# Group 0's first gates by TensorE, projection weights in three turns, and a new order of the first two groups

## The reference, cut to what matters

```python
x = x + tanh(g_xattn) * xattn(ctx, layernorm(x))        # 64 sequences of 128 tokens, 77 context tokens, width 128
h = layernorm(x)
logits = normalize(h) @ normalize(sim) - sigmoid(gates)  # 16 experts
w = softmax(where(mask > 0, relu(logits), -inf))         # mask: logits > 0, or the two largest
q, k, v = [sum_e w[:, e] * (h @ p[e]) for p in (q_proj, k_proj, v_proj)]
o = softmax(q @ k.T / sqrt(128)) @ v                     # within a sequence
x = x + tanh(g_ffn) * sum_e w[:, e] * (o @ o_proj[e])
```

## Time and profile before

| | us |
|---|---|
| median of 3 runs | 800.32 |
| lowest and highest | 799.54, 801.37 |
| the profiled execution | 799.99 |
| its span | 798.1 |
| TensorE busy | 776.1 (97%) |
| VectorE busy | 607.2 (76%) |
| GpSimd busy | 483.0 (61%) |
| ScalarE busy | 433.8 (54%) |
| mean granted clock of TensorE | 0.987 of 2.4 GHz |

### The profile page before, as it was taken

One profiled execution on the slowest core, in us unless ns is written; L12 is line 12 of the kernel. 1 busy time (PEld: TensorE's weight loads), 2 busy tenths in 40 slices (PEclk: granted clock), 3 DMA queues, 4 the chain that ended last, 5 costly groups with the idle time before them and its releaser, 6 DMA issues.

```text
span 798.1 us, 13995 instructions
## 1 busy us (share of the span) xinstructions
PE 776.1 (97%) x3999; PEld 418.1 (52%) x3999; DVE 607.2 (76%) x2037; ACT 433.8 (54%) x1129; POOL 483.0 (61%) x703
## 2 busy tenths in 40 slices
PE   7489999999999999999999999999999999999998
PEld 6445545555455555545555554555555455544444
DVE  2977787878787787778777787877878786775648
ACT  5554645556555655655565565456556555544445
POOL 3276657674746757474675747567574755765534
PEclk9789999999999999999999999999999999999999
DMA  6564476563655636365563636546364654543100
GB/s 192 136 216 159 162 219 174 169 209 94 209 161 164 189 106 204 97 210 167 151 191 106 202 109 209 166 150 186 101 207 116 208 160 139 163 135 116 53 14 28
DMA packets 97476, 122.57 MB, mean 154 GB/s; under 512 B 14611, under 2 KB 69111, under 8 KB 97399
## 3 DMA queue, kind: packets, MB, share of 16 engines
q1 hardware_dynamic: 96679, 121.59, 49.6%
q10 hardware_dynamic: 720, 0.08, 0.1%
HBM read 97.32 MB, written 24.31 MB: 152 GB/s over the span
## 4 chain that ended last, share of the span: by engine, by line
PE 88%; DVE 5%; DMA 2%; POOL 1%; ACT 1%; issue 1%; SPq 0%; DVEq 0%; ACTq 0%; POOLq 0%
PE acc_q L1380 20%; PE acc_k L1380 20%; PE acc_v L1380 20%; PE y L1409 9%; PE oT_p L1409 9%; PE m L1489 2%; PE m L1553 2%; DVE x_all L1175 1%; PE oT_p L1641 1%; PE m L1480 1%; PE m L1539 1%; DMA stage<-in_L_ffn_q_proj_dram 1%; PE m L1469 1%; POOL zq L658 1%; PE m L1529 1%
## 5 line engine op out<-in xcount | busy, mean ns | idle before, releaser
L658 POOL TENSOR_TENSOR zq<-zq_full,zq 128x512 f16<-128x512 f32 x256 | 297.8, 1170 | 222.4 <-ACT zq L743 222.2
L743 ACT ACTIVATE zq<-zq_full 128x512 f16<-128x512 f32 x256 | 160.1, 636 | 224.1 <-DVE zq_full L1145 224.0
L1175 DVE SCALAR_TENSOR_TENSOR x_all<-y,w_out,x_all 128x128 f32<-128x128 f32 x356 | 122.2, 343 | 96.1 <-issue 69.5
L1380 PE MATMUL acc_q<-zq,w_hi 128*128 128x512 f16 x510 | 193.3, 379 | 1.0 <-POOL zq L658 1.0
L1380 PE MATMUL acc_k<-zq,w_hi 128*128 128x512 f16 x510 | 193.2, 379 | 0.0
L1380 PE MATMUL acc_v<-zq,w_hi 128*128 128x512 f16 x510 | 193.2, 379 | 0.0
L1145 DVE TENSOR_TENSOR zq_full<-wq_bc,x2T_p 128x512 f32<-128x512 f32 x256 | 167.8, 668 | 2.5 <-DMA wq_bc<-w_rows 1.7
L1175 DVE SCALAR_TENSOR_TENSOR x_all<-oT_p,w_out,x_all 128x128 f32<-128x128 f32 x356 | 121.5, 341 | 0.0
L673 POOL TENSOR_TENSOR x_all<-stage,x_all 128x128 f32<-128x128 f32 x240 | 100.4, 456 | 19.8 <-DVE x_all L1175 13.3
L1380 PE MATMUL acc_q<-zq,w_lo 128*128 128x512 f16 x255 | 96.6, 379 | 0.0
L1380 PE MATMUL acc_v<-zq,w_lo 128*128 128x512 f16 x255 | 96.6, 379 | 0.0
(11 more groups left out here) (253 smaller groups left out, 1091.4 us busy)
## 6 DMA issues: line engine op xcount, KB each, us to landing
wq_bc<-w_rows SPq DMA_DIRECT2D x128, 512.0 KB, 4.5
blk_rows<-stage SPq DMA_DIRECT2D x26, 256.0 KB, 2.7
stage<-blk_rows SPq DMA_DIRECT2D x104, 64.0 KB, 2.0
blk_rows<-v_blk SPq DMA_DIRECT2D x15, 256.0 KB, 2.0
v_mix<-blk_rows SPq DMA_DIRECT2D x60, 64.0 KB, 2.9
blk_rows<-pc_blk SPq DMA_DIRECT2D x15, 256.0 KB, 4.1
pcT<-blk_rows SPq DMA_DIRECT2D x60, 64.0 KB, 2.0
out_dram<-x_all SPq DMA_DIRECT2D x15, 256.0 KB, 6.7
```

The source lines that it names most:

```text
L658: nc.gpsimd.tensor_tensor(zq[:, 1, e % Z_SLOTS, :], zq_full[:, e % F_SLOTS, :], zq[:, 0, e % Z_SLOTS, :], ALU.subtract).then_inc(zq_lo_poo ...
L743: nc.scalar.activation(zq[:, 0, e % Z_SLOTS, :], zq_full[:, e % F_SLOTS, :], ACT.Copy).then_inc(zq_hi_done, 1)
L1175: nc.vector.scalar_tensor_tensor(out=rows(x_all, g, b0 + b), in0=bank[:, tok(j)], scalar=w_out[:, g % 2, e, b0 + b:b0 + b + 1], in1=rows(x ...
L1380: last = nc.tensor.matmul(acc[m][:], w[:, m, s, :], zq[:, half, s % Z_SLOTS, :], start=(s == 0 and n == 0), stop=(s == E - 1 and n == 2))
```

## The change

1. *Gates by TensorE.* For the experts 0 and 1 of group 0 (BY_PE = 2) `gate_diagonal` on VectorE builds a 128x512 tile with the gates on the diagonal of each 128x128 block, in wq_bc's slot 0, and `gate_spread` multiplies it by a matrix of ones: the gates then stand in every partition, in the banks m0 and oT_p. `zq_scale` reads them there, with x2T from SBUF. SyncE's spread of pair 0 is left out.
2. *Weights in three turns.* Q, K, V are split for experts 0 to 3, 4 to 9 and 10 to 15 (PARTS) in instructions of their own; the last turn is in pass 0. TensorE waits for each turn where its first expert comes, and `first_expert` does its three w_hi products ahead of the w_lo ones.
3. *The head's order.* The cross-attention of group 0 goes ahead of the transposes of contexts 1 to 3; Q's weights are loaded ahead of those contexts, x of group 1 ahead of V's weights. The statistics of group 1's first norm come sooner, and the gates of group 0 are ahead of the weights' scales. More, shorter runs of `keep_busy` stand between the head's products. `att_product(1)` and `x1_add(1)` go into pass 0.
4. *Pass 0.* The second norm of group 1 moves (x2_norm at step 3, its transpose and gates two steps later than before: GATES_LATE = 3); `second_rstd(1)`, `second_norm(1)` and `first_rstd(2)` on POOL move behind more of group 0's zq_low; x_norm(2) goes to step 4 and its transpose to bank m1.
5. *O's weights* are looked through and split later: maximum at step 10 instead of 2, shared at 11 and 12 instead of 4 and 7, w_hi at step 14 instead of 9, w_lo at step 3 of pass 1 instead of step 11 of pass 0. In pass 1 the copy of oT goes ahead of that step's zq_high.

The diff, cut:

```diff
+BY_PE = 2
+PARTS = ((0, 4), (4, 10), (10, 16))
+GATES_LATE = 3
...
         def late(i):
-            return 1 if i == 0 else 0
+            return GATES_LATE if i == 0 else 0
...
-        MAX_AT, SHARE_AT = (0, 2), ((0, 4), (0, 7))
-        HIGH_AT = (0, 9)
-        LOW_AT = (0, 11)
+        MAX_AT, SHARE_AT = (0, 10), ((0, 11), (0, 12))
+        HIGH_AT = (0, 14)
+        LOW_AT = (1, 3)
...
                 sp.wait_ge(kq_in, 16 * 2)
+                load_weights(Q, q_proj)
...
-                load_weights(Q, q_proj)
                 load_weights(K, k_proj)
+                load_x(1)
                 load_weights(V, v_proj)
-                load_x(1)
...
-                for j in range(W_SLOTS):
+                for j in range(BY_PE // 2, W_SLOTS):
                     spread_q(0, j)
...
                 first_rstd(1)
-                for e in range(LEAD - 1):
+                for e in range(LEAD):
                     zq_low(0, e)
-                second_rstd(1)
-                zq_low(0, LEAD - 1)
-                first_rstd(2)
...
+                    if i == 0 and s == 2:
+                        second_rstd(1)
                     for g, e in zq_at(i, s):
                         zq_low(g, e)
-                    if s == 1 and i < 2:
+                    if s == (3 if i == 0 else 1) and i < 2:
                         second_norm(g2)
+                    if i == 0 and s == 3:
+                        first_rstd(2)
...
+                    if i == 1 and s == Y_FIRST:
+                        oT_high(0)
+                    if i == 0 and s == 3:
+                        x2_norm(1)
                     for g, e in zq_at(i, s):
                         zq_high(g, e)
...
-                    if s == (3 if i == 0 else 0) and has(g1):
+                    if s == (4 if i == 0 else 0) and has(g1):
                         x_norm(g1)
...
+                    if i == 0 and s in (1, 2, 3):
+                        weight_high((Q, K, V)[s - 1], 2)
-                    if s == 1 and i < 2:
+                    if s == 1 and i == 1:
                         x2_norm(g2)
...
+            def gate_diagonal(e):
+
+                wait(dve, w_ready, 1)
+                nc.vector.tensor_tensor(wq_bc[:, 0, e].rearrange("p (b t) -> p b t", b=G),
+                                        ident[:].unsqueeze(1).broadcast_to([P, G, P]),
+                                        w_new[:, 0, e].unsqueeze(2).broadcast_to([P, G, P]),
+                                        ALU.mult).then_inc(w_diag_done, 1)
...
+                if g == 0 and e < BY_PE:
+                    wait(dve, x2T_sb, 1)
+                    wait(dve, w_spread_ps, e + 1)
+                    nc.vector.tensor_tensor(zq_full[:, e, :], SPREAD_BANKS[e][:], x2T[:],
+                                            ALU.mult).then_inc(zq_full_done, 1)
+                    return
...
+                    if i == 0 and s == 0:
+                        x1_add(1)
+                        second_stats(1)
+                        weight_low(V, 1)
+                    if i == 0 and s == 2:
+                        first_stats(2)
+                    if i == 0 and s in (3, 4, 5):
+                        weight_low((Q, K, V)[s - 3], 2)
...
-                wait(pe, logit_read, cap(g))
+                if g == 2:
+                    wait(pe, x1_done, 2)
...
+            def gate_spread(e):
+
+                pe.wait_ge(w_diag_done, e + 1)
+                pe.wait_ge(logit_read, 1)
+                nc.tensor.matmul(SPREAD_BANKS[e][:], ones[:], wq_bc[:, 0, e], start=True,
+                                 stop=True).then_inc(w_spread_ps, 1)
...
+                px_transpose(0)
+                att_product(0)
                 for g in range(1, PRE + 1):
                     ctx_transpose(g)
...
+                keep_busy(6)
+                gate_spread(0)
+                gate_spread(1)
                 px_transpose(1)
-                att_product(1)
+                keep_busy(2)
...
+                    if i == 0 and s == 0:
+                        att_product(1)
```

More of the change, by code:

```diff
@@ L971, in body @@
                         kxT_out(g1)
[L972 to L975 removed]
+                    if s == Y_FIRST and i > 1 and has(gc):
+                        oT_high(gc)
                     if s == 10 - sooner(i) and has(g1):
@@ L1376, in experts @@
                 for m in (Q, K, V):
+                    for part, (first, _) in enumerate(PARTS):
+                        if (i, s) == (0, first):
+                            pe.wait_ge(hi_done[m], part + 1)
+                            pe.wait_ge(lo_done[m], part + 1)
                     if s == 0:
```

109 lines of the change are left out of this document (62 added, 47 removed).

## The result

The changed kernel takes **810.23 us** (median of 4 executions, 808.72 to 811.24) against 800.83 (4 executions, 799.54 to 801.37) on the same chip: ratio 1.0118, 95% interval 1.0094 to 1.0142. Slower, as forecast, but by 9.4 us and not 5, and outside the range. The profiled execution took 809.29 us, 9.30 more than the profiled one of before.

The account below looks back on a forecast made before the run. TensorE bounds the kernel, busy 776.1 of 798.1 us, with time to win only in the first 43 us. Terms -7.1, +1.0, +5.4, +3.2, +1.4, +0.5, +0.7 sum to +5.1: 805.0 us, chance 0.50, range 799.8 to 807.5.

Parts of the forecast that it names:

- to expert 0: Head and gates by TensorE: gates ready at 32.3, spread 0.9 and diagonal 0.6 each; expert 0 at 36.1, 7.1 us earlier.
- 5 to 6: Norm of group 1: second_rstd(1) behind zq_low 5, TensorE idle 1.6 us for x2_norm(1); expert 6 at 53.9, 5.2 earlier.
- 6 to 7: Norm of group 2: first_rstd(2) late on POOL, TensorE waits 4.5 us in xn_transpose(2); expert 7 only 0.7 earlier.
- 7 to 12: Out's weights: maximum behind group 1's gate chain, waits of 2.7 and 1.2 us; expert 12 at 74.8, 2.5 later.
- I take 0.7, since VectorE's chain, not TensorE, sets expert 12: Clock behind the 4.5 us wait of TensorE: a fall to half clock, costed at 0.7 us.
- The upper bound of 1.7: Highest cost of the clock's fall, for a stretch with 3.4 us of matmuls; the other upper bound was 1.2.
- The sentence on the Trainium skill's rule: Throttled state is the default and activity releases it; by that the wait costs its full 1.7, the sum 1.0 higher.
- An operation of VectorE with both inputs in SBUF and a zq_low don't run together: VectorE and POOL among group 0's zq_low: the later one waits; expert 0 waits 0.5 and 1.5 for first w_lo pieces.
- rival (a): VectorE and POOL overlap freely, the exclusion doesn't bite: 800.5 us, up to 801.7 with the clock; chance 0.20.
- rival (b): Lead survives xn_transpose(2) if first_rstd(2) is done by 54.2, before second_norm(1): -1.5 to -3.5, 797.5 us; chance 0.13.
- Rival (c): Clock falls in the head too, or the pair by DMA lands late: +6.5 to +8, 807 us; chance 0.17.
- Rival (d): Diagonal brings nothing, as V's first w_lo piece and the pair by DMA set the pace; changes no time, no chance given.

Follow-up runs that it names:

- e6: Changed kernel with the w_lo pieces for Q, K and V reading x2T_p in PSUM instead of w_hi in SBUF; 807.92 us, ratio to before 1.0092.
- e1: Changed kernel with 10 short float32 products ahead of TensorE's wait for x2 of group 1 and 20 ahead of that for xn of group 2; 807.61 us.
- e2: Changed kernel with second_rstd(1) and first_rstd(2) earlier on POOL, x2_norm(1) and x_norm(2) one step earlier on ScalarE; 802.70 us, ratio to before 1.0030.
- e3: Changed kernel with the four places of out's weights (maximum, share, high half, low half) as before; 804.14 us, ratio to before 1.0044.
- e5: Changed kernel with the edits of e2 and e3 together; 802.08 us, ratio to before 1.0020.
- e10: e5 without the diagonals and float32 spreads, all of group 0's gates by DMA as before; 803.38 us, ratio to before 1.0043.
- e9: e5 with the transpose of wmax, and out's share, high and low half, two steps later; 801.30 us, ratio to before 1.0008.
- e13: e9 with the six later w_lo pieces computing 128 of 768 columns, the other low halves zero; 797.79 us, ratio to before 0.9973.
- e14: e9 with GATES_LATE = 2, second_norm(1) one step sooner and the last w_lo pieces one later; 800.27 us, ratio to before 0.9997.
- e12: e9 with 27 more short float32 products filling TensorE's waits in the head, among the experts and in group 2; 800.84 us, ratio to before 1.0013.
- e11: Kernel before with the early activation of oT for group 0 and 46 more short float32 products in the head; 801.81 us, ratio to before 1.0019.
- e4: Changed kernel with 12 more short float32 products in the head, ahead of px's transpose, the attention product and the contexts' transposes; 809.82 us, ratio to before 1.0115.
- e8: e5 with each weight's halves split whole, in one turn of 16 experts instead of three; 804.34 us, ratio to before 1.0056.

## Why the prediction was right in sign and wrong in size

By its own steps, walk against the two profiles (us, minus is earlier than before):

| step | walk | measured | what failed |
|---|---|---|---|
| to expert 0 | -7.1 | -6.15 | gates 0.7 later than 32.3, a spread 1.12 for 0.9, a diagonal 0.65 |
| expert 0 to 1 | +1.0 | +0.77 | |
| 1 to 5 | -0.5 | -0.58 | |
| 5 to 6 | +1.4 | +2.98 | wait 2.5 for 1.6, second_rstd(1) held up by w_lo (e6: +1.59); clock 0.4 (e1: +2.57) |
| 6 to 7 | +4.5 | +5.24 | xn of group 2 comes later still, second_norm(1) 2.2 for 1.57; not the clock (e1: +5.23) |
| 7 to 12 | +3.2 | +4.64 | expert 7 at half clock, 4.79 (e1, at full clock: +2.99) |
| 12 to group 1 | +1.4 | +1.48 | |
| to group 2 | +0.5 | +0.99 | xnT late by 1.7 for 1.4; oT gave back 0.8 |
| clock | +0.7 | in the steps | fell three times, not once |
| sum | +5.1 | +9.37 | |

The miss of 4.3 us is thus 0.95 in the head, 1.6 and 0.7 at the two norms, 1.4 behind expert 7 and 0.3 in the other steps, less the 0.7 that the walk had set aside for the clock. e1 and e6 put their share of it between expert 0 and group 2 at 1.4 us for the clock and 1.7 for the exclusion, from one profile each.

*Right*, and shown by a run that undoes each: the lead dies in the norms (e2: 7.5 us of the median come off with the order of the norms), and at out's weights (e3: 6.1 us). The two overlap and don't add (8.2 together), so neither figure is a share of the loss. The exclusion of VectorE and POOL is real (e6), and group 2 carries the lag to the end. The places, and most durations, were those of the walk.

*Wrong: the clock.* The step "I take 0.7, since VectorE's chain, not TensorE, sets expert 12" failed. The runs show 1.4 to 2.6 us in its place (e1), for two falls among the experts. The upper bound of 1.7 took a stretch of 3.4 us of products at half clock, a length that no row shows; behind the second wait it was 5.7 (62.81 to 68.51). There TensorE was itself the chain: the logits of group 1 ride on expert 7, and VectorE stood idle for 8.2 us until they came. The reading behind the term was off as well: before's clock was not at 1.00 until 28.85, its trace has 0.50 from 12 to 15 us too. The sentence on the Trainium skill's rule ("TensorE: Matmul & The Clock Gate", section "What's actually happening") gave a sum 1.0 higher; the trace lies nearer to it than to mine, though not even it reaches the result.

*Wrong: what w_lo holds up.* "An operation of VectorE with both inputs in SBUF and a zq_low don't run together" was applied to zq_low alone. The power and the products of the norms on POOL, four elements wide, wait in the same way: 1.0 us on second_rstd(1), directly in the wait for x2(1), which became 2.5, and 0.6 on second_norm(1), in the chain to xn of group 2. With the exclusion off (e6) the step from expert 5 to 6 is +1.59, near the walk's +1.4.

*Wrong: the head*, by 0.95. The terms for the diagonal and the spread were near. In the profiles with this head expert 0 starts between 36.5 and 39.2, depending on where the half clock falls (last section), a fall that the walk did not have.

*Wrong: the price of rival (a)*, 800.5. With the exclusion switched off for Q, K and V (e6) the time is 807.9. The rival's walk let everything else fall into place; it did not.

*Right for a wrong reason: rival (b)* named the one place that decides, first_rstd(2) ahead of second_norm(1). e2 makes that true, the lead passes to expert 7 (20.68 us behind expert 0, 18.25 in before, so that 1.7 of the lead is left there), and the time is 802.7, not 797.5. What is left was not in the rival: e2 still has out's weights behind the gate chain (with them back, e5, 802.1) and VectorE's extra work.

*Rival (c)*, the clock falling in the head too, was the true case as far as it went (0.68 to 0.83 from 15 to 22 us), but its 807 was 3 short for the reasons above. *Rival (d)* falls: with the later steps mended, the kernel without the diagonals (e10) is 1.3 us slower than the one with them (e5).

Of what would show it right, the longest wait stood in the transpose of xn (3.5 instead of 4.5), 1.9 ahead of the transpose of wmax, none above 1 on oT, two zq_low took 3.63, and the clock stood at 0.50 around 63.

*What stays open*: of the 5.6 us that e9 takes longer than before from expert 0 to group 2, e13 removes 2.3, e14 0.3; the rest is not pinned to one cause. Nor is the scatter of the times of e5 and e12, though the start of expert 0 alone moves by 2.6 us between profiles (last section).

## What to carry to other kernels

A lead on the bounding engine is worth what the feeding engines can follow: compare each feeder's busy time from the new start to the next stage with what it was, before costing the lead. Where a change moves a small operation behind large ones on another queue, its whole chain counts, and a wait of 2 to 3 us on TensorE can be paid twice, once as idle time and once as half clock behind it, unless the next wait takes the second payment up (e1). Products that fill a wait help where the wait stands among the experts (e1) and harm where they delay a short operation on the path (e11).

## What the runs showed that was not expected

*The clock fell with TensorE busy.* In e11 it was granted at 0.50 from 30.6 to 33.6 while TensorE was busy for 8.00 of 8.00 us around it, with 128-column float32 products; its last wait, of 0.67 us, had ended at 27.86. (In e4 the fall came around a wait of 1.0 us and is no such case.) The Trainium skill's rule ("TensorE: Matmul & The Clock Gate", section "What's actually happening") that activity releases the throttle agrees with e1, where the same products held it at 1.00; it doesn't explain e11, and what was different there no run here tells.

*Half pace at a granted clock of 1.00.* In e9 the record of the clock has 1.00 from 7 us on (first fence: windows of e9), but the products of the head run at half the pace they have in the changed kernel, the eight score products in 1.99 us instead of 1.12 (second fence: TensorE's timeline in e9; third: in the changed kernel):

```profile
8.00:12.00 4.00, 3.17 (x11) 1.00 0.68 186
12.00:19.40 7.40, 6.48 (x28) 1.00 1.05 276
```

```profile
11.84 1.99 PE L1539 MATMUL m<-kxT,xnT 128*128 128x77 f32 x8 [0.69 <-ACT xnT L829]
```

```profile
10.96 1.12 PE L1539 MATMUL m<-kxT,xnT 128*128 128x77 f32 x8 [0.69 <-ACT xnT L829]
```

So early in an execution the durations of equal instructions tell the pace better than the clock's row. It was so in the profiles of e2, e5, e8 and e9.

*Where the head runs at half pace decides when expert 0 starts.* The stretch at half pace lies elsewhere in each profile. In e5 it ended ahead of the product of px, which took 1.16 us at 17.00; in e9 it went on, the same product took 2.08 at 17.59. The transpose of group 0's x, which stands behind the contexts' products, then starts at (first line e5, second e9):

```profile
24.39 0.66 PE L1560 MATMUL m<-ident,x 128*128 128x128 f32 x4 [0.32 <-ACT x L798]
```

```profile
27.06 0.66 PE L1560 MATMUL m<-ident,x 128*128 128x128 f32 x4 [0.16 <-ACT x L798]
```

Expert 0 follows 12.08 to 12.13 us behind this transpose in the profiles of the changed kernel, e1, e2, e3, e5, e6, e9 and e14, wherever it starts. So the 2.6 us between 36.52 (e5) and 39.15 (e9) arise ahead of it, in TensorE's pace. Whether this also scatters the times of a kernel's executions is not shown.
